# Graph network, last two layers: steps of 50 places in five blocks, and edge jobs spread over more groups

## The chip, the cores and the metric

One core of a Trainium2 chip runs the whole program. The metric is device microseconds of one execution, the median of several. Before the change it is 16802.36 us (three executions, 16799.04 to 16803.32).

## The reference

12500 nodes with 48 features pass four graph layers over the same 400000 edges (sorted by destination); each layer's result is added to the features and normalized.

```
x = ln(x + L0)   # message MLP on [x_dst, x_src, edge], summed over dst
x = ln(x + L1)   # x_src * deg^-1/2, summed over dst, linear, relu
x = ln(x + L2)   # deg^-1/2 scaled x_dst, summed over SRC, linear, relu
x = ln(x + L3)   # gate(edge) * x_dst * cutoff * mult, summed over SRC, divided
# gate(edge) = silu(edge_attr_40 @ W1 + b1) @ W2 + b2 + adapt(edge)
```

The last two layers sum over the source node, by which the edges are not sorted.

## The kernel before, in words

The edges are cut into 125 groups of 3200 (25 tiles of 128, in five chunks). Layers 0 and 1 (`pass0`, `pass1`) go over them once each. `pass0` also counts how many edges go to each block of 128 source nodes, one count for each of six *parts* of the groups (`GROUPS`). `pass1` works out a place for every edge in a table `order` in DRAM, in which, part by part, the edges of one block of nodes lie together. The places are read later in *steps* of `RT` = 40, a place being 128 rows; for each step DVE works out which blocks of nodes its places belong to (`block_no`, called numbering here, L1179 to L1181, once for each of the first 40 groups, and L1265 to L1270 after them).

Layers 2 and 3 are both `scatter_pass` (L1570). For each group:

- SP loads ids, five windows of the node table and the edge data (`load_edges`).
- DVE builds one-hots of the destinations (L1825); PE looks the 25 tiles up with 25 small matmuls (L1940, `look_up`).
- ACT (`begin`) writes the message tile and the places (L2030 to L2032) once the scatters of the same chunk of the group before have landed; DVE multiplies (`take`: L1844 in layer 2, L1841 in layer 3). In layer 3 ACT makes the gates of reading groups itself, 25 activations (L2020), from coefficients of DVE (L1814, L1817).
- POOL scatters the 25 tiles to `order` (L1757), one indirect DMA each.

The first part (40 groups) does this and, beside it, the *jobs*: a job is the gate network over one group of 3200 edges (PE L1913 and L1920, ACT L1992 and L1999, stored to `gates`). `GATES2` and `GATES3` say for each layer how many groups carry two jobs (*pairs*), how many carry one (*singles*), and the first job. The pass asserts that the jobs take `GROUPS[0] - 1` groups. Layer 2 makes jobs 0 to 77 in 39 groups, layer 3 makes 78 to 124 in 8 + 31.

From the second part on, each group also reads one step (*reading groups*): SP loads the step's places, one DMA for each block of 10 places (`load_order`, L1685), each after PE has reduced the same block of the step before. DVE builds the one-hots of a block (`block_digits`, L1789), PE reduces the ten places into one of two PSUM banks, `red[b % 2]` (`block_reduce`: L1904 clears, L1906 multiplies), and DVE adds the bank to the node sums (`block_sums`, L1803). DVE's order in a group is: one-hots for the look-up, the sum of the last block of the step before, then the five products, with a block's one-hots built behind each of the first four, then the other sums. PE does the look-up and then the step's blocks. The first group of each part is a *head*: SP waits until all scatters of the parts before have landed, then loads; DVE builds after all products. When the groups are through, the steps that are left (nine) run as a *tail*.

Of the kernel before, what the change touches and what calls it, by code (L numbers as in the profile page):

```python
# [41 lines left out]
MW = F + 1  # L42
# [2 lines left out]
BANK = 512  # L45
AHEAD = 3
ROUND_BIT = 512
GROUPS = (40, 28, 20, 15, 12, 10)
PARTS = len(GROUPS)
OW = MW + 1  # L50
RB = (10, 10, 10, 10)
LINE = 16
RT = sum(RB)
TEN = RB[0]
RUN = 10
GATES2 = (39, 0, 0)
GATES3 = (8, 31, 78)


class Plan:  # L60


    def __init__(self, n, e):
# [7 lines left out]
        assert self.NR <= ROUND_BIT  # L71
        assert sum(GROUPS) == self.NG
        self.begin = [sum(GROUPS[:q]) for q in range(PARTS)]
        self.TAIL = -(-(GROUPS[-1] * GT + self.NB) // RT)
        self.steps = GROUPS[1:] + (self.TAIL,)
        self.step0 = [sum(self.steps[:q]) for q in range(PARTS)]
        assert all(n * GT + self.NB <= k * RT for n, k in zip(GROUPS, self.steps))
        self.NS = sum(self.steps)
# [22 lines left out]
def bc(ap, shape):  # L101
    return ap.to_broadcast(shape)


def gnn(nc, a, out):
# [4 lines left out]
    def dram(name, shape, dt=F32):  # L110
# [16 lines left out]
        order=dram("order", [P * pl.TT, OW]),  # L127
        blocks=dram("blocks", [pl.NS, len(RB) + 1, LINE], I32),
    )
# [826 lines left out]
def pass1(nc, pl, a, d, r, ps):  # L956
# [5 lines left out]
    NG, NB, TT, HB = pl.NG, pl.NB, pl.TT, pl.HB  # L962
    MOST = max(pl.steps)
    ADDS = SC + DT
    assert GROUPS[0] == RT
    hacc = ps[0:F, 0:SC * WN].rearrange("p (c n) -> p c n", n=WN)
    cumf = ps[:, BANK:BANK + CT * NB]
    cum = cumf.rearrange("p (t b) -> p t b", b=NB)
# [9 lines left out]
    with Stage(nc, "l1") as s:  # L978
# [33 lines left out]
        block_no = s.sb("block_no", [MOST, PARTS, RT])  # L1012
        blk = s.sb("blk", [MOST, PARTS, len(RB) + 1, LINE], I32)
        first_of = s.sb("first_of", [MOST, PARTS * len(RB)])
        zero = s.sb("zero", [P, pl.ZT * OW])
# [12 lines left out]
        blk_ready, blk_out = s.sem("blk_ready"), s.sem("blk_out")  # L1028
        first_found, blk_made = s.sem("first_found"), s.sem("blk_made")
# [67 lines left out]
        def _(dve):  # L1097
            v = nc.vector
# [60 lines left out]
                    more = hacc[:, i, :] if i < SC else packed[:, (i - SC) * WD:(i - SC + 1) * WD]  # L1159
                    v.tensor_tensor(cols, cols, more, ALU.add).then_inc(acc_added, 1)  # L1160

            def group(g, part):
                mine = ids[:, ds(g % 2, 1), :, :].rearrange("p o t k -> p (o t) k")
                dve.wait_ge(ids_in, (g + 1) * 16)
                dve.nop(nofuse=True)
# [9 lines left out]
                v.scalar_tensor_tensor(near[:, :], nodes[:, ST:GT], 16.0, r["dbase"][:, ds(g, 1), :].rearrange("p o t -> p (o t)"), ALU.mult, ALU.subtract).then_inc(self_id, 1)  # L1175
                v.scalar_tensor_tensor(far[:, 0:ST].rearrange("p (c t) -> p c t", t=CT), nodes[:, 0:ST].rearrange("p (c t) -> p c t", t=CT), 4.0,
                                       bc(base4[:, ds(g, 1), :].rearrange("p o c -> p c o"), [P, SC, CT]), ALU.mult, ALU.subtract).then_inc(self_id, 1)
                if part == 0:
                    v.tensor_tensor(begun[:, :, :], first_tile[0:MOST, :, :], bc(tile_no[0:MOST, ds(g, 1)].rearrange("p (q o) -> p q o", o=1), [MOST, PARTS, NB]), ALU.is_le).then_inc(self_blk, 1)  # L1179
                    dve.wait_ge(self_blk, g + 1)  # L1180
                    v.tensor_reduce(block_no[:, :, ds(g, 1)].rearrange("p q o -> p (q o)"), begun[:, :, :], AX, ALU.add).then_inc(blk_ready, 1)  # L1181
# [76 lines left out]
                dve.wait_ge(self_shift, last * 2 + 3)  # L1258

            dve.wait_ge(lone_set, len(batches))  # L1260
            for part in range(PARTS):
                if part == 1:
                    dve.wait_ge(blk_ready, RT)
                    tens = block_no[:, :, :].rearrange("p q (b k) -> p (q b) k", k=TEN)
                    v.tensor_scalar(first_of[:, :], tens[:, :, 0], float(MW), None, ALU.mult).then_inc(first_found, 1)  # L1265
                    dve.wait_ge(first_found, 1)
                    for q in range(PARTS):
                        mine = slice(q * len(RB), (q + 1) * len(RB))
                        v.scalar_tensor_tensor(blk[:, q, 0:len(RB), 0:TEN], tens[:, mine, :], float(MW), bc(first_of[:, mine].rearrange("p (b o) -> p b o", o=1), [MOST, len(RB), TEN]), ALU.mult, ALU.subtract)
                        v.tensor_scalar(blk[:, q, len(RB), 0:len(RB)], first_of[:, mine], float(-MW), None, ALU.add).then_inc(blk_made, 1)  # L1270
                    dve.wait_ge(blk_made, PARTS)
                    dve.sem_inc(blk_ready, 1)
                with dve.Fori(pl.begin[part], pl.begin[part] + GROUPS[part]) as g:
                    group(g, part)
            with dve.Fori(NG - 1, NG) as g:
                _bodies, _before, last = load_bodies(dve, "dve", pl, r, g)
                add_sums(last + 1)
# [292 lines left out]
def scatter_pass(nc, pl, a, d, r, ps, layer):  # L1570
# [7 lines left out]
    NG, NB, NT, TT = pl.NG, pl.NB, pl.NT, pl.TT  # L1578
# [3 lines left out]
    HE = EV * P  # L1582
    pairs, singles, job0 = (GATES3 if gated else GATES2)
    JOBS = pairs + singles
# [23 lines left out]
    STEP = len(RB)  # L1608
# [3 lines left out]
    with Stage(nc, f"l{layer}") as s:  # L1612
# [10 lines left out]
        blk = s.sb("blk", [1, 2, STEP + 1, LINE], I32)  # L1623
# [19 lines left out]
        ohs_ready, red_ready, agg_added = s.sem("ohs_ready"), s.sem("red_ready"), s.sem("agg_added")  # L1643
# [245 lines left out]
        @block.tensor  # L1889
        def _(pe):  # L1890
            t = nc.tensor
            pe.sem_inc(look_ready, 5)
            pe.sem_inc(win_used, 2)
            pe.sem_inc(red_ready, len(RB))
            pe.sem_inc(z_ready, 2 * NCH)
            pe.wait_ge(zeros_set, 1)

            def block_reduce(n, b):
                pe.wait_ge(ohs_ready, n * len(RB) + b + 1)
                pe.wait_ge(ord_in[b], (n + 1) * 16)  # L1900
                pe.wait_ge(blk_in, (n + 2) * 16)
                slots = load_slots(pe, "slot", r, blk, n, b)
                pe.wait_ge(agg_added, n * STEP + b + STEP)
                t.matmul(red[b % 2], none[:, 0:P], none[:, :], start=True, stop=False, skip_group_check=True)  # L1904
                for k in range(TEN):
                    done = t.matmul(red[b % 2][:, ds(slots[k], MW)], ohs[b][:, k, :],  # L1906
                                    ordb[b][:, k, 0:MW], start=False, stop=False, skip_group_check=True)
                done.then_inc(red_ready, 1)

            def make_hidden(g, many, i):  # L1910
                pe.wait_ge(ea_in[i // NCH][i % NCH], (g + 1) * 16)
                pe.wait_ge(sil_ready, item0(g, many) + i + 1)
                t.matmul(zps, w1[:, :], eat[:, i // NCH, i % NCH, :], start=True, stop=True).then_inc(z_ready, 1)  # L1913

            def make_gates(g, many, i):
                pe.wait_ge(sil_ready, item0(g, many) + i + 2)
                pe.wait_ge(made_copied, item0(g, many) + i + 1)
                for q in range(EV):
                    wide = F * min(2, CT - 2 * q)
                    done = t.matmul(gps[:, 2 * q * F:2 * q * F + wide], sil[:, i % 2, q * P:(q + 1) * P], w2[:, 0:wide], start=True, stop=True)  # L1920
                done.then_inc(made_ready, 1)

            def jobs(g, many):
                make_hidden(g, many, 0)
                for i in range(many * NCH):
                    if i + 1 < many * NCH:
                        make_hidden(g, many, i + 1)
                    make_gates(g, many, i)

            def look_up(g):  # L1930
                _starts, rounds, before, last_round = load_group(pe, "pe", pl, r, g)
                with pe.Fori(0, rounds) as k:
                    w = before + k
                    n = w * NCH
                    pe.wait_ge(win_in, (w + 1) * 16 * NCH)
                    for c in range(NCH):
                        pe.wait_ge(oht_ready, n + c + 1)
                        pe.wait_ge(look_zero, g * NCH + c + 1)
                        for j in range(CT):
                            done = t.matmul(look[c][:, j, :], oht[:, c * CE + j * P:c * CE + (j + 1) * P],  # L1940
                                            win[:, ds((w % 2) * SET + c * LW, LW)], start=False, stop=False, skip_group_check=True)
                        done.then_inc(look_ready, 1)
                    pe.wait_ge(look_ready, n + NCH + 5)
                    pe.sem_inc(win_used, 1)

            with pe.Fori(0, 1) as g:
                look_up(g)
            pe.wait_ge(w_in, 8 * 16)
            for begin, end, many in spans:
                with pe.Fori(begin + 1, end + 1) as g:  # L1950
                    look_up(g)
                    jobs(g - 1, many)
            assert JOBS + 1 == READ0
            pe.wait_ge(made_copied, (2 * pairs + singles) * NCH + 1)
            with pe.Fori(READ0, NG) as g:
                look_up(g)
                for b in range(len(RB)):
                    block_reduce(g - READ0, b)
            with pe.Fori(NG - READ0, pl.NS) as n:
                for b in range(len(RB)):  # L1960
                    block_reduce(n, b)
# [486 lines left out]
```

## Time and profile before

| what | value |
|---|---|
| median of the runs | 16802.36 us |
| profiled execution, its own time | 16791.52 us |
| its span | 16789.7 us |
| PE, PEld (share of the span) | 69%, 57% |
| DVE, ACT | 52%, 23% |
| POOL | 66% |
| mean granted clock | 0.661 |

Layer 2 goes from about 7815 to 12224 us of the span, layer 3 from about 12310 to 16700. The shares are averages over four layers and their epilogues, so the rows below are taken stretch by stretch. A timeline row gives the start of an instruction and, in brackets, how long its engine was idle before it and what released it.

### The profile page before, as it was taken

To read this page: it belongs to the slowest core of one execution; us is meant where nothing else is said; L and a number is where in the kernel's file an instruction comes from. 1 tells how busy PE (TensorE), PEld (TensorE's weight loads), DVE (VectorE), ACT (ScalarE), POOL (GpSimd) and SP (SyncE) were. 2 spreads that over 40 slices of the span, in tenths; PEclk is the share of its full clock that TensorE was granted. 3 is DMA by queue.
4 is the path that set the end of the run, shared out by engine and by line. 5 is a ranking of instruction groups with operands and counts; after the bars stand their busy time and mean duration, and the time that the engine had idled before them with its cause. 6 is when DMAs were issued, how large, how long until landed. Compare 5 with 4: busy or idle time off the path is not lost. (4 is left out here: it accounts for less than half of the span.)

```text
span 16789.7 us, 290124 instructions
## 1 busy us (share of the span) xinstructions
PE 11513.4 (69%) x64352; PEld 9568.8 (57%) x64353; DVE 8750.1 (52%) x19588; ACT 3873.3 (23%) x10408; POOL 11073.3 (66%) x11400
## 2 busy tenths in 40 slices
PE   7877877877666666665777766666755446666666
PEld 6777777777444444444555666566643336565555
DVE  4666666666677666664111444444432234444444
ACT  1111111111222222223444211111022223333331
POOL 4777777777545555555666777777546777777773
PEclk9999999999766666665555555555555555555555
DMA  5444444443111111112333333333223333333331
GB/s 130 101 101 101 101 100 101 102 101 91 47 40 43 45 46 44 46 44 76 110 110 110 95 87 87 86 84 90 71 77 92 94 92 95 88 96 92 92 92 51
DMA packets 1579142, 1406.93 MB, mean 84 GB/s; under 512 B 987004, under 2 KB 1445903, under 8 KB 1574658
## 3 DMA queue, kind: packets, MB, share of 16 engines
q1 hardware_dynamic: 601532, 636.68, 14.5%
q0 software_dynamic: 410000, 462.80, 11.0%
q10 hardware_dynamic: 567508, 306.27, 6.6%
q8 instruction: 42, 0.69, 0.0%
q14 instruction: 60, 0.49, 0.0%
HBM read 984.49 MB, written 420.17 MB: 84 GB/s over the span
## 5 line engine op out<-in xcount | busy, mean ns | idle before, releaser
L1757 POOL DMA_INDIRECT order<-l_msg,l_uring x6250 | 6069.5, 971 | 2356.7 <-issue 1831.9
L547 POOL DMA_INDIRECT l_rows<-btab,l_sd x3125 | 2993.7, 958 | 1128.3 <-issue 1087.2
L1906 PEld LDWEIGHTS ps<-l_ordb,l_ohs 128*128 128x128 f32 x15040 | 3263.7, 331 | 313.8 <-issue 313.8
L1906 PE MATMUL ps<-l_ordb,l_ohs 128*128 128x49 f32 x15040 | 3385.3, 415 | 0.0
L1086 POOL DMA_INDIRECT l_rows<-y,l_sd x1875 | 1822.0, 972 | 1621.5 <-DMA l_sd<-in_sd 1087.9
L688 PE MATMUL ps<-l_rhs,l_lhs 64*128 x6250 | 1421.9, 424 | 666.5 <-DVE l_rows L624 466.5
L688 PEld LDWEIGHTS ps<-l_rhs,l_lhs 64*128 64x128 f32 x6250 | 1350.8, 328 | 728.1 <-issue 728.1
L1904 PE MATMUL ps<-l_none 1*128 1x490 bf16 x752 | 438.0, 582 | 1694.4 <-DVE l_ohs L1789 1143.1
L1071 ACT ACTIVATE l_adj<-ps 128x588 f16<-128x588 f32 x1260 | 784.0, 664 | 2636.3 <-PE ps L1315 2629.0
L703 PEld LDWEIGHTS ps<-l_ohe,l_hid 128*128 128x128 f32 x6250 | 1342.8, 332 | 34.7 <-issue 34.0
L703 PE MATMUL ps<-l_ohe,l_hid 128*128 128x32 f32 x6250 | 1359.8, 402 | 0.6 <-ACT l_hid L733 0.6
L733 ACT ACTIVATE l_hid<-l_rows 128x640 f32<-128x640 f32 x625 | 460.4, 737 | 3509.6 <-DVE l_rows L624 3509.6
L1940 PE MATMUL ps<-l_win,l_oht 96*128 x6250 | 474.8, 243 | 1158.7 <-DVE l_oht L1825 912.9
L1334 PEld LDWEIGHTS ps<-l_adj,yhm 128*96 128x96 f16 x12348 | 941.3, 173 | 545.9 <-DVE acc L1160 408.0
L1315 PE MATMUL ps<-l_okey,l_hlo 128*128 128x294 bf16 x2520 | 680.7, 390 | 795.2 <-DVE l_okey L1202 636.8
L1803 DVE TENSOR_TENSOR acc<-acc,ps 128x490 f32 x752 | 500.9, 666 | 1328.9 <-PE ps L1906 1170.9
L1334 PE MATMUL ps<-l_adj,yhm 128*96 128x60 f16 x12348 | 940.3, 247 | 345.6 <-DVE acc L1160 345.6
L1920 PEld LDWEIGHTS ps<-l_w,l_sil 97*128 97x128 f32 x3750 | 924.8, 329 | 440.5 <-issue 382.4
L1789 DVE TENSOR_TENSOR l_ohs<-ps,l_ordb 128x1280 f32<-128x1280 f32 x752 | 1113.1, 1481 | 69.7 <-DMA l_ordb<-order 69.5
L1844 DVE TENSOR_TENSOR l_prod<-ps,l_esr 128x160 f32<-128x160 f32 x625 | 200.8, 322 | 1819.2 <-ACT l_uring L2032 1685.5
L1940 PEld LDWEIGHTS ps<-l_win,l_oht 96*128 96x128 bf16 x6250 | 401.4, 132 | 1240.3 <-issue 1238.0
L1904 PEld LDWEIGHTS ps<-l_none 1*128 1x128 bf16 x752 | 74.0, 98 | 1782.9 <-issue 1223.0
(317 smaller groups left out, 15842.4 us busy)
## 6 DMA issues: line engine op xcount, KB each, us to landing
l_ordb<-order SPq DMA_DIRECT2D x752, 250.0 KB
l_dstb<-ids SPq DMA_DIRECT2D x250, 600.0 KB
order<-l_msg,l_uring POOLq DMA_INDIRECT x6250
order<-l_zero ACTq DMA_DIRECT2D x125, 775.0 KB
l_eat<-in_ea40P SPq DMA_DIRECT2D x625, 120.0 KB, 2.1
gates<-l_made ACTq DMA_DIRECT2D x625, 120.0 KB
l_gin<-gates SPq DMA_DIRECT2D x125, 600.0 KB
l_rows<-btab,l_sd POOLq DMA_INDIRECT x3125
```

Source lines behind the costliest of these rows:

```text
L547: pool.indirect_dma_start(rows[:, t, :], None, d["btab"], bass.IndirectOffsetOnAxis(ap=sd[:, t, 0:1], axis=0)).then_inc(gat[c], 16)
L688: last = t.matmul(pre[c % 2][:, j * P:(j + 1) * P], lhs[:, c * CE + j * P:c * CE + (j + 1) * P], window, start=True, stop=True)
L703: last = t.matmul(hacc[:, c, :], hid[:, c * CT + j, :], ohe[:, c * CT + j, :], start=(j == 0), stop=(j == CT - 1))
L1071: nc.scalar.activation(adj[:, :, t * WD:(t + 1) * WD].rearrange("p (h n) d -> p h n d", n=HB), pair[t % 2].rearrange("p h (n d) -> p h n d ...
L1086: pool.indirect_dma_start(rows[:, slot, t, :], None, d["y1"], bass.IndirectOffsetOnAxis(ap=sd[:, slot, t, 0:1], axis=0)).then_inc(gat[c], 16)
L1315: done = t_.matmul(pair[t % 2][:, h, :], hlo[:, t % BUILT, :], okey[:, t % BUILT, h * HB * WD:(h + 1) * HB * WD], start=True, stop=True)
L1334: done = t_.matmul(packed, r["yhm"][:, b, :], adj[:, b, :], start=(b == 0), stop=(b == NB - 1))
L1757: pool.indirect_dma_start(d["order"], bass.IndirectOffsetOnAxis(ap=uring[:, t:t + 1], axis=0), msg[:, t, :], None).then_inc(sc[c], 16)
L1789: v.tensor_tensor(ohs[b][:, :, :], bc(count_row[:, None, :], [P, RB[b], P]), bc(lo, [P, RB[b], P]), ALU.is_equal).then_inc(ohs_ready, 1)
L1906: done = t.matmul(red[b % 2][:, ds(slots[k], MW)], ohs[b][:, k, :], ordb[b][:, k, 0:MW], start=False, stop=False, skip_group_check=True)
L1920: done = t.matmul(gps[:, 2 * q * F:2 * q * F + wide], sil[:, i % 2, q * P:(q + 1) * P], w2[:, 0:wide], start=True, stop=True)
L1940: done = t.matmul(look[c][:, j, :], oht[:, c * CE + j * P:c * CE + (j + 1) * P], win[:, ds((w % 2) * SET + c * LW, LW)], start=False, stop ...
```

## The change

The constants become `GROUPS = (54, 29, 17, 11, 8, 6)`, `RB` five blocks of 10, so `RT` = 50, `GATES2 = (19, 34, 0)` and `GATES3 = (0, 53, 72)`.

- Layers 2 and 3 have 54 groups before reading in place of 40, and 71 reading groups in place of 85, each with a step of five blocks; the steps of the parts are 29, 17, 11, 8, 6 and 5 (76 in all; 94 before: 28, 20, 15, 12, 10 and 9), so the tail has five steps in place of nine. A layer reads 380 blocks in place of 376.
- Layer 2 makes 72 jobs: 19 groups with two, 34 with one. Layer 3 makes 53, one a group.
- The fifth block's one-hots are built behind the fifth product. As the number of blocks is now odd, the first block of a step has the same bank as the last of the step before, and PE waits for one more sum there.
- There is one more buffer for places and one for one-hots.
- `pass1` numbers the first 50 groups, and DVE's loop over the groups is split there alone and no longer at every part.

```diff
--- before.py
+++ after.py
@@ -45,16 +45,16 @@
 BANK = 512
 AHEAD = 3
 ROUND_BIT = 512
-GROUPS = (40, 28, 20, 15, 12, 10)
+GROUPS = (54, 29, 17, 11, 8, 6)
 PARTS = len(GROUPS)
 OW = MW + 1
-RB = (10, 10, 10, 10)
+RB = (10, 10, 10, 10, 10)
 LINE = 16
 RT = sum(RB)
 TEN = RB[0]
 RUN = 10
-GATES2 = (39, 0, 0)
-GATES3 = (8, 31, 78)
+GATES2 = (19, 34, 0)
+GATES3 = (0, 53, 72)
 
 
 class Plan:
@@ -962,7 +962,7 @@
     NG, NB, TT, HB = pl.NG, pl.NB, pl.TT, pl.HB
     MOST = max(pl.steps)
     ADDS = SC + DT
-    assert GROUPS[0] == RT
+    assert RT <= GROUPS[0]
     hacc = ps[0:F, 0:SC * WN].rearrange("p (c n) -> p c n", n=WN)
     cumf = ps[:, BANK:BANK + CT * NB]
     cum = cumf.rearrange("p (t b) -> p t b", b=NB)
@@ -1159,7 +1159,7 @@
                     more = hacc[:, i, :] if i < SC else packed[:, (i - SC) * WD:(i - SC + 1) * WD]
                     v.tensor_tensor(cols, cols, more, ALU.add).then_inc(acc_added, 1)
 
-            def group(g, part):
+            def group(g, numbering):
                 mine = ids[:, ds(g % 2, 1), :, :].rearrange("p o t k -> p (o t) k")
                 dve.wait_ge(ids_in, (g + 1) * 16)
                 dve.nop(nofuse=True)
@@ -1175,7 +1175,7 @@
                 v.scalar_tensor_tensor(near[:, :], nodes[:, ST:GT], 16.0, r["dbase"][:, ds(g, 1), :].rearrange("p o t -> p (o t)"), ALU.mult, ALU.subtract).then_inc(self_id, 1)
                 v.scalar_tensor_tensor(far[:, 0:ST].rearrange("p (c t) -> p c t", t=CT), nodes[:, 0:ST].rearrange("p (c t) -> p c t", t=CT), 4.0,
                                        bc(base4[:, ds(g, 1), :].rearrange("p o c -> p c o"), [P, SC, CT]), ALU.mult, ALU.subtract).then_inc(self_id, 1)
-                if part == 0:
+                if numbering:
                     v.tensor_tensor(begun[:, :, :], first_tile[0:MOST, :, :], bc(tile_no[0:MOST, ds(g, 1)].rearrange("p (q o) -> p q o", o=1), [MOST, PARTS, NB]), ALU.is_le).then_inc(self_blk, 1)
                     dve.wait_ge(self_blk, g + 1)
                     v.tensor_reduce(block_no[:, :, ds(g, 1)].rearrange("p q o -> p (q o)"), begun[:, :, :], AX, ALU.add).then_inc(blk_ready, 1)
@@ -1258,20 +1258,20 @@
                 dve.wait_ge(self_shift, last * 2 + 3)
 
             dve.wait_ge(lone_set, len(batches))
-            for part in range(PARTS):
-                if part == 1:
-                    dve.wait_ge(blk_ready, RT)
-                    tens = block_no[:, :, :].rearrange("p q (b k) -> p (q b) k", k=TEN)
-                    v.tensor_scalar(first_of[:, :], tens[:, :, 0], float(MW), None, ALU.mult).then_inc(first_found, 1)
-                    dve.wait_ge(first_found, 1)
-                    for q in range(PARTS):
-                        mine = slice(q * len(RB), (q + 1) * len(RB))
-                        v.scalar_tensor_tensor(blk[:, q, 0:len(RB), 0:TEN], tens[:, mine, :], float(MW), bc(first_of[:, mine].rearrange("p (b o) -> p b o", o=1), [MOST, len(RB), TEN]), ALU.mult, ALU.subtract)
-                        v.tensor_scalar(blk[:, q, len(RB), 0:len(RB)], first_of[:, mine], float(-MW), None, ALU.add).then_inc(blk_made, 1)
-                    dve.wait_ge(blk_made, PARTS)
-                    dve.sem_inc(blk_ready, 1)
-                with dve.Fori(pl.begin[part], pl.begin[part] + GROUPS[part]) as g:
-                    group(g, part)
+            with dve.Fori(0, RT) as g:
+                group(g, True)
+            dve.wait_ge(blk_ready, RT)
+            tens = block_no[:, :, :].rearrange("p q (b k) -> p (q b) k", k=TEN)
+            v.tensor_scalar(first_of[:, :], tens[:, :, 0], float(MW), None, ALU.mult).then_inc(first_found, 1)
+            dve.wait_ge(first_found, 1)
+            for q in range(PARTS):
+                mine = slice(q * len(RB), (q + 1) * len(RB))
+                v.scalar_tensor_tensor(blk[:, q, 0:len(RB), 0:TEN], tens[:, mine, :], float(MW), bc(first_of[:, mine].rearrange("p (b o) -> p b o", o=1), [MOST, len(RB), TEN]), ALU.mult, ALU.subtract)
+                v.tensor_scalar(blk[:, q, len(RB), 0:len(RB)], first_of[:, mine], float(-MW), None, ALU.add).then_inc(blk_made, 1)
+            dve.wait_ge(blk_made, PARTS)
+            dve.sem_inc(blk_ready, 1)
+            with dve.Fori(RT, NG) as g:
+                group(g, False)
             with dve.Fori(NG - 1, NG) as g:
                 _bodies, _before, last = load_bodies(dve, "dve", pl, r, g)
                 add_sums(last + 1)
@@ -1900,7 +1900,7 @@
                 pe.wait_ge(ord_in[b], (n + 1) * 16)
                 pe.wait_ge(blk_in, (n + 2) * 16)
                 slots = load_slots(pe, "slot", r, blk, n, b)
-                pe.wait_ge(agg_added, n * STEP + b + STEP)
+                pe.wait_ge(agg_added, n * STEP + b + STEP + (1 if b == 0 and STEP % 2 else 0))
                 t.matmul(red[b % 2], none[:, 0:P], none[:, :], start=True, stop=False, skip_group_check=True)
                 for k in range(TEN):
                     done = t.matmul(red[b % 2][:, ds(slots[k], MW)], ohs[b][:, k, :],
```

## Rows read from the trace of the kernel before

**Rows 1.** Stretches: busy us (count) by engine, granted clock, DMA share, GB/s.

```profile
10500.00:11500.00 1000.00, 683.92 (x3421) 609.85 (x3420) 462.67 (x657) 155.36 (x633) 760.35 (x787) 0.50 0.32 87
15000.00:16000.00 1000.00, 673.14 (x3415) 595.10 (x3414) 455.88 (x685) 368.76 (x1336) 755.98 (x782) 0.50 0.34 92
```

**Rows 2.** Waits, layer 2 reading: us in total, times, longest.

```profile
ACT l_msg L2030 <- DMA order<-l_msg,l_uring: 1017.6, 234, 6.8
```

**Rows 3.** Timeline of POOL (start, us, what, idle before): scatters.

```profile
8530.64 0.97 POOL L1757 DMA_INDIRECT order<-l_msg,l_uring  x1 [2.57 <-ACT l_uring L2032]
...
9335.37 0.97 POOL L1757 DMA_INDIRECT order<-l_msg,l_uring  x1 [7.00 <-ACT l_uring L2032]
...
12035.52 0.97 POOL L1757 DMA_INDIRECT order<-l_msg,l_uring  x1 [0.30 <-issue]
...
13794.09 0.97 POOL L1757 DMA_INDIRECT order<-l_msg,l_uring  x1 [7.96 <-ACT l_uring L2032]
...
16511.08 0.97 POOL L1757 DMA_INDIRECT order<-l_msg,l_uring  x1 [0.30 <-issue]
```

**Rows 4.** Timeline of PE, layer 2: look-ups, two jobs between.

```profile
8528.75 1.86 PE L1940 MATMUL ps<-l_win,l_oht 96*128 x25 [7.46 <-DVE l_oht L1825]
...
8566.90 1.85 PE L1940 MATMUL ps<-l_win,l_oht 96*128 x25 [7.32 <-DMA l_win<-y]
```

**Rows 5.** Timeline of PE, layer 3: look-ups, two jobs between.

```profile
12536.28 0.39 PE L1940 MATMUL ps<-l_win,l_oht 96*128 x5 [16.29 <-DVE l_oht L1825]
...
12583.55 0.39 PE L1940 MATMUL ps<-l_win,l_oht 96*128 x5 [16.11 <-DVE l_oht L1825]
```

**Rows 6.** Timeline of PE, layer 3: look-ups, one job between.

```profile
13304.16 0.39 PE L1940 MATMUL ps<-l_win,l_oht 96*128 x5 [15.42 <-DVE l_oht L1825]
...
13338.27 0.39 PE L1940 MATMUL ps<-l_win,l_oht 96*128 x5 [15.41 <-DVE l_oht L1825]
```

**Rows 7.** Timeline of PE, layer 2: look-ups of groups behind a head.

```profile
9364.48 1.99 PE L1940 MATMUL ps<-l_win,l_oht 96*128 x25
...
9390.59 2.18 PE L1940 MATMUL ps<-l_win,l_oht 96*128 x25
```

**Rows 8.** Timeline of PE, layer 3: blocks 0, 0 and 1 behind a head.

```profile
13799.36 0.58 PE L1904 MATMUL ps<-l_none 1*128 1x490 bf16 x1 [10.66 <-DVE l_ohs L1789]
...
13828.95 0.58 PE L1904 MATMUL ps<-l_none 1*128 1x490 bf16 x1 [7.10 <-DVE l_ohs L1789]
...
13833.90 0.58 PE L1904 MATMUL ps<-l_none 1*128 1x490 bf16 x1
```

**Rows 9.** Timelines of ACT and DVE, layer 3: gates, first product.

```profile
13816.93 8.05 ACT L2020 ACTIVATE l_gate<-l_gin,l_cwa,l_cwg 128x48 f32 x25 [10.83 <-DVE l_cwa L1817]
...
13825.28 0.41 DVE L1841 TENSOR_TENSOR l_msg<-ps,l_gate 128x245 f32<-128x245 f32 x1 [2.90 <-ACT l_uring L2032]
```

**Rows 10.** Timeline of SP's queue, layer 2: first load of the tail.

```profile
12038.34 0.59 SPq L1681 DMA_DIRECT2D l_blk<-blocks  x1
```

**Rows 11.** Timelines of SP, PE, PE and POOL, layer 3: a head group.

```profile
14686.94 0.27 SPq L1681 DMA_DIRECT2D l_blk<-blocks  x1
...
14693.47 0.58 PE L1904 MATMUL ps<-l_none 1*128 1x490 bf16 x1 [24.28 <-DVE l_ohs L1789]
...
14713.12 0.69 PE L1940 MATMUL ps<-l_win,l_oht 96*128 x10
...
14720.99 0.96 POOL L1757 DMA_INDIRECT order<-l_msg,l_uring  x1 [3.73 <-ACT l_uring L2032]
```

**Rows 12.** Page, costliest groups: busy, mean ns, idle before.

```profile
L1803 DVE TENSOR_TENSOR acc<-acc,ps 128x490 f32 x752 | 500.9, 666 | 1328.9 <-PE ps L1906 1170.9
...
L1789 DVE TENSOR_TENSOR l_ohs<-ps,l_ordb 128x1280 f32<-128x1280 f32 x752 | 1113.1, 1481 | 69.7 <-DMA l_ordb<-order 69.5
```

**Rows 13.** Stretches, layer 1, DVE's line L1244 alone: ten groups each.

```profile
5073.70:5352.40 278.70, 26.99 (x10) 0.65 0.16 43
5464.60:5733.50 268.90, 27.00 (x10) 0.63 0.16 45
```

## The prediction

> **What bounds the kernel now.** I read the busy shares of stretches first, then each engine's timeline for the repeating group of 3200 edges, then the waits. In both reading stretches (groups that scatter messages and also reduce one step of the order) the granted clock is 0.50, the lower level (1.2 GHz), in layer 2 and in layer 3 alike; POOL issues 787 and 782 scatters per 1000 us, 31.8 and 32.0 us for the 25 of a group [rows 1]. In layer 2 ACT waits 234 times for a scatter's landing before it may write the message tile again [rows 2]: the others run ahead and are held back by POOL. From first to last scatter of the 85 reading groups POOL takes 2700.2 us in layer 2 (31.78 a group) and 2717.0 us in layer 3 (31.98, with the idle of the heads below) [rows 3]. Where jobs are made, POOL is not the bound: from look-up to look-up a group takes 38.15 us with two jobs in layer 2 [rows 4], 47.27 (47.0 over the eight) with two in layer 3 [rows 5], and 34.11 (34.15 over the thirty) with one in layer 3 [rows 6].
>
> What the others need when POOL does not hold them back shows right behind a head group. Layer 2: 26.11 from look-up to look-up [rows 7]. Layer 3: 29.59 from first block to first block, 4.95 between blocks [rows 8]. Layer 3 needs more because the loop goes through ACT: DVE's sum of the last but one block, coefficients, 25 gate activations (8.05 us) on ACT, the first product on DVE, its one-hots, PE's first block [rows 8, 9]. This loop has 2.3 us to spare in layer 3 and 5.7 in layer 2. The change adds a fifth block to it.
>
> **Layer 3, term by term.** (a) Jobs: eight groups of 47.0 go, 22 of 34.15 come: -376.0 + 751.3 = +375.3 us until reading begins. (b) The reading loop: one block more before the sum that starts the next group: 29.75 (mean of some thirty such groups) + 4.95 = 34.70 us. That is above POOL's 32: POOL now waits about 2.8 us in each group. (c) Heads, the first group of each part: SP holds the order loads until all earlier scatters have landed. The last scatter's end to SP's first load is 1.85 us (12036.49 to 12038.34) [rows 3, 10]; SP to the first block 6.53, four blocks 19.65 to the next look-up, 7.87 from there to POOL's first scatter [rows 11]. With five blocks: 31.57 (25 scatters) + 1.85 + 6.53 + 24.60 + 7.87 = 72.4 us over two groups where the loop alone gives 69.4: 3.0 us a head. The four-block head already shows POOL idle for 3.73 [rows 11], which this sum gives as 3.7. (d) Reading after: 70 intervals of 34.70, five heads of 3.0, the last group's 31.6: 2475.6 against 2717.0, -241.4. (e) Tail: before, nine steps of four blocks, 36 x 4.95 = 178.1 us; after, five of five, 25 x 4.95 = 123.7. The number of blocks to a step becomes odd, so block 0 uses the bank of the last block of the step before, and PE must wait for its sum: 0.67 us [rows 12]. The trace has no such wait; between 0 (hidden) and 2 us (three sums' length) I take 0.93, the sum and an estimated quarter to see it, as in the tail nothing lies between; behind it on PE stand all further blocks, and DVE's sums wait for them. Four times: +3.7. Together -50.7. Within reading the same wait costs nothing: DVE does that sum before it builds the one-hots for which block 0 waits in any case; were this cover gone, 0.9 us for each of 71 groups, 66 us a layer where PE bounds. Layer 3: +375.3 - 241.4 - 50.7 = **+83.2 us**.
>
> **Layer 2.** (a) Twenty groups with two jobs go: -763.0. (b) 34 groups with one job come, a form that layer 2 does not have in the trace. Below, POOL's 31.78 bounds them (nothing can pass it); above, the layer 3 form at 34.15. That one is a loop through the gates loaded for the next group (loads, cutoff activations, coefficients), which layer 2 has not; five jobs fewer are worth 12.9 us in layer 3 (47.0 against 34.11), so layer 2's own loop would want about 38.15 - 12.9 = 25.3. I take 31.78: +1080.5, and 2.2 us once (0 to 4, an estimate), as the first of them finds its second chunk late. (c) Before reading, the wait for the stored gates leaves POOL idle 7.00 against 2.57 in a pair group [rows 3]; behind single groups POOL has nearly a group in hand and this goes: -4.4. (d) Fourteen reading groups go: -444.9. (e) The reading loop becomes 26.11 + 4.95 = 31.06, under 31.78 by 0.7: POOL keeps the bound, thinly. (f) Heads: SP's first load to the next look-up is 6.53 + 24.60, and 1.89 to POOL [rows 3, 4], 33.0 us; POOL is free after 31.78 + 0.30 - 1.85 = 30.2: 2.8 us idle, five times, +14.0 (none with four blocks). (g) Tail -50.7. Layer 2: **-166.3 us**.
>
> The fifth load of 250 KB a step is issued by SP once PE has reduced the same block of the step before, a whole group ahead of its use. DMA share is 0.32 to 0.34 [rows 1], so a quarter more of these loads finds room; if it did not, a step would start late as it does at heads, where the loads are open: 6.53 us.
>
> **Layer 1.** Numbering runs for the first 50 groups in place of 40. DVE's ten groups take 278.7 us with it and 268.9 without [rows 13]: 0.98 a group, +9.8. PE has a loop of its own for the last group of an odd part; three parts are odd in place of one: between 0 and 6 us, I take 3. **+12.8 us**. Layer 0 keeps its six parts and its work: 0.
>
> **Sum.** -166.3 + 83.2 + 12.8 = -70.3. The profiled execution took 16791.5 (span 16789.7), so 16721.2; the median shown is 10.8 higher, so **16732 us**, 0.4% faster.
>
> **Rivals.** (A) POOL stays the bound in layer 3 as well. For it: no engine is busier there, POOL 756 against PE 673 and DVE 456 of 1000 us [rows 1]. Against it: the loop behind heads repeats at 29.6 to 30.0 with no engine full, and POOL is already idle at heads. Then 71 groups at 31.98, 2270.6 in place of 2475.6: 205 us less, 16527 us. The Trainium skill's Perfetto Trace Analysis, section Identifying the Most-Contended Engine, says the engine with the highest occupancy is the most contended and is to be optimized first; by that, work added to PE and DVE is free, which is this rival. The rows of layer 2 agree with it, those behind the heads of layer 3 do not. (B) Slower: the loop grows by more than a block, because the fifth one-hot build now stands between the last product and the first sum (1.48 us [rows 12]), and the bank wait of 0.93 is not covered. Layer 3 then goes with 37.1 us and layer 2 with 33.5: 70 x 2.4 + 71 x 1.7 = +289, 17021 us. For it: in steady state PE's third block waits for exactly that first sum. Against: PE has two blocks (9.9 us) in hand while DVE gets there. It decides from 1.0 us a group in layer 3 alone (70 us over 70 groups). (C) Layer 2's single groups are held by their loads at 34.15: 34 x 2.37 = +81, 16813 us, no change.
>
> **How the numbers follow.** Forecast 0.70, its own range 16695 to 16770 (0.3 us a group in the layer 3 loop is 21 us; layer 2's transitions 10; layer 1's odd loops 3; 10 between executions). A 0.06, B 0.09, C 0.08; the rest, 0.07, are mixtures just above the forecast. The range that leaves out A and most of B, but holds C: 16665 to 16820. What this measurement can tell from no change is 0.2%, 34 us, so the borders are 16769 and 16836. Faster: 0.68 of the forecast, A, 0.02 of the rest, 0.76. Same: C and the forecast's edge, 0.15. Slower: 0.09.
>
> **What would show it.** In the profile after: look-ups of layer 3's reading groups 34.7 apart and POOL idle about 2.8 us before each group's first scatter; layer 2's 31.8 apart with only heads showing POOL idle; layer 2's groups 20 to 53 at 31.8; PE's tails 127 us. Wrong would be: layer 3 at 32 (A), layer 2 above 32.5 (B) or at 34 before reading (C).

## The result and the profile after

The kernel after takes 16707.27 us (median of 5 runs, 16700.66 to 16713.0), the kernel before, beside it, 16799.04 us (16794.38 to 16803.32): a ratio of 0.9945, 95% interval 0.993 to 0.996. The forecast was 16732 in a range of 16665 to 16820, so the time lies 25 us below it and inside the range. The profiled execution spans 16698.9 us against 16789.7: 90.8 us less, where the sum of the prediction had 70.3.

The page after, its span and its busy shares:

```profile
span 16698.9 us, 289908 instructions
PE 11607.6 (70%) x64520; PEld 9620.9 (58%) x64521; DVE 8794.7 (53%) x19652; ACT 3819.4 (23%) x10108; POOL 11083.6 (66%) x11400
```

The shares say nothing of where the time went; the same two stretches as in [rows 1] do:

```profile
10500.00:11500.00 1000.00, 823.81 (x4024) 737.07 (x4024) 511.07 (x711) 152.75 (x620) 756.35 (x784) 0.50 0.34 94
15000.00:16000.00 1000.00, 750.11 (x3714) 666.00 (x3713) 473.58 (x687) 343.67 (x1242) 694.10 (x717) 0.50 0.34 93
```

In layer 2 POOL still issues 784 scatters per 1000 us (787 in [rows 1]), though PE has 824 us of work there in place of 684. In layer 3 it issues 717 in place of 782: a group takes 34.9 us here on average, heads included, where it took 32.0. The granted clock is 0.50 in both, the lower level, as before.

From PE's timeline in layer 2, two look-ups before reading and two behind a head:

```profile
9029.06 0.51 PE L1940 MATMUL ps<-l_win,l_oht 96*128 x5 [7.55 <-DVE l_oht L1825]
...
9060.85 0.51 PE L1940 MATMUL ps<-l_win,l_oht 96*128 x5 [7.57 <-DVE l_oht L1825]
...
9722.50 1.58 PE L1940 MATMUL ps<-l_win,l_oht 96*128 x20
...
9753.54 1.54 PE L1940 MATMUL ps<-l_win,l_oht 96*128 x20
```

A group with one job takes 31.79 us: POOL's pace. Behind a head, where POOL does not hold it back, a reading group takes 31.04; in [rows 7] it was 26.11.

From POOL's timeline, the first scatter of reading, a first group behind a head, and the last scatter of layer 2; then the first of reading, two group starts and the last of layer 3 (before: [rows 3]):

```profile
9659.02 0.97 POOL L1757 DMA_INDIRECT order<-l_msg,l_uring  x1 [0.30 <-issue]
...
9693.25 0.97 POOL L1757 DMA_INDIRECT order<-l_msg,l_uring  x1 [2.76 <-ACT l_uring L2032]
...
11926.45 0.97 POOL L1757 DMA_INDIRECT order<-l_msg,l_uring  x1 [0.30 <-issue]
...
13999.96 0.97 POOL L1757 DMA_INDIRECT order<-l_msg,l_uring  x1 [8.13 <-ACT l_uring L2032]
...
14071.94 0.97 POOL L1757 DMA_INDIRECT order<-l_msg,l_uring  x1 [3.19 <-ACT l_uring L2032]
...
14106.66 0.97 POOL L1757 DMA_INDIRECT order<-l_msg,l_uring  x1 [3.18 <-ACT l_uring L2032]
...
16471.40 0.97 POOL L1757 DMA_INDIRECT order<-l_msg,l_uring  x1 [0.31 <-issue]
```

Layer 2 reads for 2267.4 us (before 2700.2), layer 3 for 2471.4 (before 2717.0). In layer 3 POOL waits 3.2 us before every reading group outside heads (0.3 in before). One turn of layer 3's loop, from the timelines of DVE, ACT and PE (the block that starts at 14059.50 is the fifth of its step):

```profile
14061.99 0.19 DVE L1817 TENSOR_TENSOR l_cwa<-l_cwg,adapt 128x25 f32<-128x25 f32 x1
...
14071.09 1.48 DVE L1789 TENSOR_TENSOR l_ohs<-ps,l_ordb 128x1280 f32<-128x1280 f32 x1
...
14062.41 8.05 ACT L2020 ACTIVATE l_gate<-l_gin,l_cwa,l_cwg 128x48 f32 x25 [15.85 <-DVE l_cwa L1817]
...
14039.72 0.58 PE L1904 MATMUL ps<-l_none 1*128 1x490 bf16 x1 [7.49 <-DVE l_ohs L1789]
...
14059.50 0.58 PE L1904 MATMUL ps<-l_none 1*128 1x490 bf16 x1
14064.32 0.62 PE L1940 MATMUL ps<-l_win,l_oht 96*128 x10
...
14074.43 0.58 PE L1904 MATMUL ps<-l_none 1*128 1x490 bf16 x1 [7.49 <-DVE l_ohs L1789]
```

PE has the look-up done by about 14067 and then stands for 7.49 us, ACT had stood for 15.85 us before its gates: neither is full, each waits for the other through DVE. The first block of this step started at 14039.72, that of the next at 14074.43, so a turn is 34.71 us, and the rows account for all of it: four blocks on PE 19.78, the sum and the coefficients 2.91, the gates 8.05, and 3.97 for the first product, its one-hots and the start of PE's block. The look-up lies beside the gates.

### The profile page after: what moved, and what is told of

Read it like the earlier page. It is cut to its first block and busy times, and to the rows that moved or that the text cites. A ratio compares the mean times of both kernels' runs of the same rounds, so it can differ in the third digit from the quotient of the medians.

```text
span 16698.9 us, 289908 instructions
## 1 busy us (share of the span) xinstructions
PE 11607.6 (70%) x64520; PEld 9620.9 (58%) x64521; DVE 8794.7 (53%) x19652; ACT 3819.4 (23%) x10108; POOL 11083.6 (66%) x11400
## 5 line engine op out<-in xcount | busy, mean ns | idle before, releaser
L1906 PEld LDWEIGHTS ps<-l_ordb,l_ohs 128*128 128x128 f32 x15200 | 3298.2, 331 | 317.1 <-issue 317.1
L1906 PE MATMUL ps<-l_ordb,l_ohs 128*128 128x49 f32 x15200 | 3421.1, 415 | 0.0
L703 PEld LDWEIGHTS ps<-l_ohe,l_hid 128*128 128x128 f32 x6250 | 1342.8, 332 | 34.7 <-issue 34.0
L1789 DVE TENSOR_TENSOR l_ohs<-ps,l_ordb 128x1280 f32<-128x1280 f32 x760 | 1124.8, 1481 | 37.2 <-DMA l_ordb<-order 36.8
L1913 PE MATMUL ps<-l_eat,l_w 80*96 80x384 f32 x1250 | 987.6, 894 | 198.4 <-ACT l_sil L1992 125.3
L1825 DVE TENSOR_TENSOR l_oht<-ps,l_dstb 96x640 bf16<-96x640 f32 x1250 | 936.2, 812 | 188.1 <-DMA l_dstb<-ids 98.4
```

The source lines that it names most:

```text
L703: last = t.matmul(hacc[:, c, :], hid[:, c * CT + j, :], ohe[:, c * CT + j, :], start=(j == 0), stop=(j == CT - 1))
L1789: v.tensor_tensor(ohs[b][:, :, :], bc(count_row[:, None, :], [P, RB[b], P]), bc(lo, [P, RB[b], P]), ALU.is_equal).then_inc(ohs_ready, 1)
L1825: v.tensor_tensor(oht[:, chunk_edges(c)], bc(nid[:, c:c + 1], [WK, CE]), dstb[:, ds((g % 2) * GE + c * CE, CE)], ALU.is_equal).then_inc(oh ...
```

## The experiments

All kernels but e2 are edits of the kernel after. e1 to e4 ran on one chip, on which the kernel before takes 16809.6 us. The other three batches came to three other chips, on which it takes 23940 (e5 to e8), 24112 (f1 to f3) and 23935 us (g1); the times of a batch can be set only against runs of the same batch and that kernel, which ran in each. The times expected for them, but for a few said to be for the slow chip, were worked out for a chip like the first, so they are not tested; what is tested is how look-ups move.

**e1: ACT's gates out of the loop.**

```
# DVE, reading groups of layer 3; coefs(g) is the lines of cwg and cwa, which leave the
# start of the group; ... marks what is left out
...
+                        if gated and ahead and b == 1:
+                            coefs(g + 1)
                         block_sums(n, b)
...
# in heads the same two lines stand ahead of block_digits(n, b + 1)
```

> The kernel after, with one change in layer 3's reading groups: DVE computes the coefficients of the next group behind its first sum of a step, not behind the fourth, so the 25 gate activations no longer stand in the loop sum, coefficients, gates, product, one-hots, block 0. My theory (this loop sets layer 3's 34.7 us a group, POOL could do 31.8): the look-ups of layer 3's reading groups come to 31.8 apart, POOL's idle before each first scatter goes except at heads, its 71 reading groups take 70 x 31.78 + 5 x 2.8 + 31.6 = 2270 in place of 2472 us, and the kernel 16707 - 202 = 16505 us (16485 to 16530). Rival 1 (five blocks need this time on PE, in the loads of the order or in the one-hots, and the gates only fill a gap): look-ups stay at 34.7, 16707 us. Rival 2 (part of it): another wait, near 33, 16600 us.

Measured: 16547.71 us (16538.81 to 16549.93), 0.9846 of before (0.983 to 0.9863). That is 0.99% of the old time, about 166 us, under the kernel after, each taken against its own runs of before. PE's look-ups behind a head, ACT's gates in the group between, and what the head itself shows on PE, DVE and POOL:

```profile
15034.63 1.23 PE L1950 MATMUL ps<-l_win,l_oht 96*128 x20
...
15053.15 8.05 ACT L2030 ACTIVATE l_gate<-l_gin,l_cwa,l_cwg 128x48 f32 x25 [0.98 <-DVE l_cwa L1812]
...
15065.30 1.26 PE L1950 MATMUL ps<-l_win,l_oht 96*128 x20
...
14958.51 0.58 PE L1914 MATMUL ps<-l_none 1*128 1x490 bf16 x1 [5.14 <-issue]
...
14955.09 0.19 DVE L1809 SCALAR_TENSOR_TENSOR l_cwg<-l_under,l_cut 128x25 f32<-128x25 f32 x1 [5.85 <-ACT l_cut L1998]
...
14976.75 0.97 POOL L1757 DMA_INDIRECT order<-l_msg,l_uring  x1 [9.58 <-issue]
```

The same gates now lie beside PE's blocks, and the free loop is 30.67 us in place of 34.7. POOL's 31.8 is the bound again. The 8.05 us of gates give back 4.0 and not 8: from the end of the last sum but one to the first product it is 10.38 us in after and 6.34 in e1, since DVE's one-hots of the look-up (3.74 us) now stand where the gates stood. The time missed my 16505 by 43 us and lies above its range (to 16530), and the rows say where: my edit made a wait of its own. In a head DVE asks for the next group's cutoff before it builds the third block's one-hots, but SP loads the distances for it only behind the head's order loads; DVE stands 5.85 us, PE's third block 5.14, and POOL is idle for 9.58, 9.79, 9.90 and 10.41 us at four heads, some 28 us more than the 2.8 each of the sum. The groups before reading took 34.22 in this run and not 34.01: 11 us. The two make 39 of the 43.

**e2: the same edit with four blocks** (in the kernel before).

> The same edit in the kernel before (four blocks). My theory (with four blocks the loop is 29.75 and POOL's 31.78 the bound): only the 3.7 us of POOL idle at each of the heads of layer 3 can go, 5 x 3.7 = 19 us: 16780 us, look-ups 31.8 apart as before. Rival (layer 3's reading was bound by the loop before too): 85 groups get shorter by more than 1 us, under 16700 us.

Measured: 16807.24 us (16802.6 to 16826.01), ratio 1.000 (0.9991 to 1.001), where 16780 was expected. PE's look-ups behind a head, and POOL at that head:

```profile
14768.97 0.83 PE L1950 MATMUL ps<-l_win,l_oht 96*128 x15
...
14794.88 0.83 PE L1950 MATMUL ps<-l_win,l_oht 96*128 x15
...
14746.80 0.97 POOL L1757 DMA_INDIRECT order<-l_msg,l_uring  x1 [4.42 <-issue]
```

The free loop falls from 29.6 to 25.9 us, and nothing comes of it, since POOL had been the bound at 31.8 all along. The 19 us expected at heads stayed away too: POOL's idle there is 4.4 to 5.1 us, by the same new wait as in e1, and not 0.

With e1 this makes a table of the free loop of a reading group in layer 3, in us:

| | four blocks | five blocks | a block adds |
|---|---|---|---|
| gates in the loop | 29.6 (before) | 34.7 (after) | 5.1 |
| gates beside it | 25.9 (e2) | 30.7 (e1) | 4.8 |
| the gates cost | 3.7 | 4.0 | |

Only one of the four lies above POOL's 31.8, and it is the kernel after.

**e3: the larger step alone.**

```
-GROUPS = (54, 29, 17, 11, 8, 6)
+GROUPS = (40, 28, 20, 15, 12, 10)
...
-GATES2 = (19, 34, 0)
-GATES3 = (0, 53, 72)
+GATES2 = (39, 0, 0)
+GATES3 = (8, 31, 78)
...
-    assert RT <= GROUPS[0]
```

> The step of five blocks alone: the kernel after with the groups 40, 28, 20, 15, 12, 10 and the jobs' numbers of the kernel before, so 85 groups read and the steps are partly empty. My theory: layer 3's reading goes from 2717 to 84 x 34.65 + 5 x 2.4 + 31.6 = 2954 us, +237; tail of 7 steps of five blocks (35) for 9 of four (36), +1; layer 2 keeps POOL's 31.78 and gets 2.8 us at each of five heads and 1 in the tail, +15; layer 1 +7: 16799 + 260 = 17059 us. Rival A (the fifth block is free under POOL in both layers): +20, 16819 us. Rival B (the loop grows by more than a block): layer 3 above 36, over 17170 us.

Measured: 17073.75 us (17064.69 to 17082.47), ratio 1.0157 (1.014 to 1.0174), 264 us slower than before where 260 were expected. Two look-ups of layer 3:

```profile
15021.95 0.62 PE L1939 MATMUL ps<-l_win,l_oht 96*128 x10
...
15056.67 0.62 PE L1939 MATMUL ps<-l_win,l_oht 96*128 x10
```

34.72 apart; layer 2's free look-ups are 30.7 to 31.0 apart, and from its first look-up to that of layer 3 it takes 4539 us, where the kernel before has 4506. So a fifth block by itself is a loss; by the table of terms further down, what makes the change a gain are the fourteen fewer groups that pay for blocks at all, and the shorter tails. A first part of 54 groups with steps of four blocks was not run, so what that part is worth without the fifth block stays open.

**e4: the jobs packed as before.**

```
-GATES2 = (19, 34, 0)
-GATES3 = (0, 53, 72)
+GATES2 = (39, 0, 0)
+GATES3 = (8, 31, 78)
...
# and loops of PE and ACT for the groups from JOBS + 1 up to READ0, without a job
```

> The kernel after with the jobs as they were before: layer 2 two jobs in each of groups 0 to 38 and none in 39 to 53, layer 3 two in each of 0 to 7, one in 8 to 38 and none in 39 to 53. My theory: layer 2 pays 20 x (38.15 - 31.78) = +127 us, layer 3 8 x (47.0 - 34.0) - 14 x (34.0 - 31.8) = +73 us: 16707 + 200 = 16907 us, slower than the kernel before. Groups without a job in layer 3 then show 31.8 from look-up to look-up (a rival: 34 there too, by the loads and not by the job; then 16940). Rival: spreading the jobs is worth nothing by itself, 16707 us.

Measured: 16918.58 us (16915.34 to 16921.96), ratio 1.0067 (1.005 to 1.0084), so 1.2% (some 205 us) over the kernel after, and slower than the kernel before. Layer 3's groups without a job:

```profile
13833.33 0.39 PE L1940 MATMUL ps<-l_win,l_oht 96*128 x5 [28.89 <-DMA l_win<-htab]
...
13865.49 0.39 PE L1940 MATMUL ps<-l_win,l_oht 96*128 x5 [28.92 <-DMA l_win<-htab]
```

They are 32.2 apart, and POOL is idle for no more than 0.31 us before any of their scatters (of 0.98 us each): without a job POOL sets the pace in layer 3 as well. Spreading the jobs is the half of the change without which it would lose.

**e5: the fifth one-hots built later.**

```
-                    if reading and not head and c <= LAST:
+                    if reading and not head and c < LAST:
                         block_digits(n, c)
 ...
                         block_sums(n, b)
+                        if b == 0:
+                            block_digits(n, LAST)
```

> The kernel after, but in reading groups the one-hots of the fifth block are built behind DVE's first sum and not between the last product and that sum. My theory (the build, 1.48 us, ends when PE's block 0 of the step ends, and costs nothing): look-ups stay 34.7 apart in layer 3 and the time stays at 16707 us (+-10). Rival B (the fifth build delays the first sum, by it PE's third block, and so the loop): 1 us or more a group comes back in layer 3, under 16640 us.

Measured: 24464.98 us (24411.94 to 24472.63), 1.022 of before (1.0203 to 1.0237) on that chip. As a test of rival B this run settles nothing, for the kernel after did not run there. This part of B is settled by rows of the kernel after, DVE in two successive groups:

```profile
14043.24 1.48 DVE L1789 TENSOR_TENSOR l_ohs<-ps,l_ordb 128x1280 f32<-128x1280 f32 x1
14045.11 0.67 DVE L1803 TENSOR_TENSOR acc<-acc,ps 128x490 f32 x1 [0.39 <-PE ps L1906]
...
14077.95 1.48 DVE L1789 TENSOR_TENSOR l_ohs<-ps,l_ordb 128x1280 f32<-128x1280 f32 x1
14079.59 0.67 DVE L1803 TENSOR_TENSOR acc<-acc,ps 128x490 f32 x1 [0.16 <-PE ps L1906]
```

Behind the fifth build DVE still waits, 0.39 and 0.16 us, for PE's block 0: the build fits, with almost nothing to spare.

**e6 and f3: more gates in the loop** (the same kernel twice).

```
# ACT, reading groups of layer 3
                         make_gates(c)
+                        if c == 0:
+                            make_gates_again()   # five more, into a tile of their own
```

> The kernel after with five more gate activations on ACT in each of layer 3's 71 reading groups, behind the first five; their results go to a tile that nobody reads. Each takes 0.32 us, 1.6 us a group. My theory (ACT's gates stand in the loop that sets 34.7 us): though ACT is busy for a third of this stretch only, 71 x 1.6 = +114 us: 16821 us, look-ups 36.3 apart. But only chunk 0's gates stand between coefficients and the first product if DVE may start with it; as the extra ones stand right behind chunk 0's, the first product may go ahead and only the later ones slip: then less, at the least 0. Rival (PE's blocks or the loads of the order set 34.7): 16707 us.

> The kernel of e6 (after, with five more gate activations in each of layer 3's reading groups) once more. On a chip where the kernel before takes 16800: 71 x 1.61 = +114 us against after, 16821 us, look-ups 36.3 apart (the late chip showed 56.7 for 55.0, +1.65); rival (not ACT's gates but PE's blocks or the loads set 34.7): 16707 us.

Measured: 24564.34 us (24538.15 to 24574.72), 1.0257 (1.024 to 1.0274), 99 us over e5 on the same chip, and in the other batch 24631.91 us, 1.0216 (1.0199 to 1.0233). Two look-ups of layer 3, of e5 and then of e6:

```profile
21328.59 1.12 PE L1939 MATMUL ps<-l_win,l_oht 96*128 x15
...
21383.71 1.12 PE L1939 MATMUL ps<-l_win,l_oht 96*128 x15
```

```profile
21301.26 1.12 PE L1941 MATMUL ps<-l_win,l_oht 96*128 x15
...
21357.97 1.12 PE L1941 MATMUL ps<-l_win,l_oht 96*128 x15
```

55.1 and 56.7. Over 22 groups the means are 54.96 and 56.69, 1.73 apart; over all reading groups outside heads they are 54.95 and 56.48, 1.53 apart: about the five gates (1.61). So ACT's gates lie in the loop that sets the pace there as well, though it is 20 us longer on that chip. One thing is mixed in: e5 stands for the kernel after, from which it differs by the place of the fifth build, and what that is worth there no run shows. That the first product might leave early did not happen: it also waits for chunk 0's indices, which ACT writes in begin(0), behind all gates.

**e7 and f1: heads mended** (again one kernel).

```
# DVE, heads of layer 3; reading groups as in e1
                         block_digits(n, b + 1)
+                        if gated and ahead and b == LAST - 1:
+                            coefs(g + 1)
                         block_sums(n, b)
```

> Early coefficients as in e1, but in head groups DVE computes them ahead of its fourth sum and not of the third block's one-hots. In e1 DVE waited 5.85 us at a head for the next group's cutoff, whose load SP issues only behind the head's order loads, with PE's third block behind it, and POOL was idle for 9.6 to 10.4 us at four of the heads. My theory: that wait goes, POOL is idle for about 2.8 us at a head as in layer 2, 16548 - 5 x 7 = 16513 us (16500 to 16530). Rival (the heads are long because PE's blocks and the loads need that): 16548 us.

> The kernel of e7 (early coefficients, at heads ahead of the fourth sum) once more, since e5 to e8 ran on a chip whose transfers land so much later that the kernel before takes 23940 us there. On a chip where it takes 16800: 16513 us (16500 to 16530), look-ups of layer 3's reading groups 31.8 apart on average, POOL idle for about 2.8 us at a head. On the late chip: 24186 us again.

Measured: 24186.07 us (24136.86 to 24189.91), 1.0103 (1.0086 to 1.012), 279 us under e5; and 24268.65 us, 1.0067 (1.005 to 1.0083). Reading groups are 51.2 apart where e5 has 55.0: 3.8 us, the price of the gates in the table again. Whether the mended head brings the 35 us over e1 was not measured on a chip like that of e1 and stays open.

**e8, f2 and g1: the distances loaded early as well** (one kernel, three batches).

```
# e7, and in load_edges, right behind the load of dstb (the old load of dist goes)
+                if gated:
+                    sp.dma_start(dist[...], a["dist"][...]).then_inc(dist_in, 16)
...
# ACT's cut_weights; SP waits for dist_in too, behind its loads
-                act.wait_ge(edge_in, (g + 1) * EDGE)
+                act.wait_ge(dist_in, (g + 1) * 16)
```

> As e7, and in layer 3 the distances of a group are loaded ahead of its windows under a semaphore of their own, so that cutoff, coefficients and the look-up's one-hots no longer wait for the gates' load behind the windows. My theory (groups that make one job in layer 3 take 34.0 because of that chain, POOL would do 31.8): look-ups of groups 1 to 53 come to 31.8 apart, 53 x 2.2 = -117 us against e7: 16396 us (16380 to 16430). Rival (they are held by the job's own chain through PE and ACT, or by the windows' load): 34 stays, 16513 us.

> The kernel of e8 (the distances loaded early as well) once more. On a chip where the kernel before takes 16800: groups 1 to 53 of layer 3 at 31.8 in place of 34.0, 53 x 2.2 = 117 us less than f1: 16396 us (16380 to 16430); rival (the job's chain or the windows' load holds them): no difference to f1. On the late chip they went from 55.6 to 47.6.

> The kernel of e8 and f2 (after, with early coefficients and early distances in layer 3) for a chip where the kernel before takes 16800. Against e1 (16548): POOL's idle at heads falls from 10 to about 2.8 us, 5 x 7 = -35 us, and groups 1 to 53 of layer 3 go from 34.2 to 31.8 apart, 53 x 2.4 = -127 us: 16386 us, ratio 0.975 (0.973 to 0.980). Rival for the second term (the job's chain or the windows' load holds these groups at 34): 16513 us, ratio 0.983. On the late chip again 0.995 to 0.997.

Measured: 23811.95 us, 0.9946 (0.9929 to 0.9963); 24041.69 us, 0.997 (0.9959 to 0.9982); 23813.85 us, 0.9942 (0.9925 to 0.9959). Look-ups of layer 3's groups with one job, of e7 and then of e8:

```profile
18941.50 0.39 PE L1950 MATMUL ps<-l_win,l_oht 96*128 x5 [23.41 <-DVE l_oht L1828]
...
18996.02 0.39 PE L1950 MATMUL ps<-l_win,l_oht 96*128 x5 [20.50 <-DVE l_oht L1828]
```

```profile
18777.57 1.69 PE L1955 MATMUL ps<-l_win,l_oht 96*128 x25 [25.76 <-DMA l_win<-htab]
...
18825.05 1.67 PE L1955 MATMUL ps<-l_win,l_oht 96*128 x25 [26.61 <-DMA l_win<-htab]
```

54.5 and 47.5 us (means 55.3 and 47.6; 53.5 and 47.7 from the twentieth group on in f1 and f2): PE no longer waits for one-hots that stand behind the cutoff, but for the windows. So on these chips the chain of loads and cutoff does hold these groups, against the rival; what is left is the windows' load, which the rival had named too. On a chip like that of e1, where POOL's 31.8 would be the floor, it wasn't measured. For the slow chip g1 expected 0.995 to 0.997 and got 0.9942, with 0.995 inside the interval.

Of the kernels tried, e1 is the fastest where before takes 16800 us (0.9846, against the 0.9945 of the kernel after). On the three other chips the one of e8, by 0.3 to 0.6%, is the only one that beats before; the kernel after itself did not run on them.

## Why the prediction was right

Term by term, from the profiled executions, in us:

| | predicted | measured |
|---|---|---|
| layers 0 and 1 (to layer 2's first look-up) | +12.8 | +7.2 |
| layer 2 until reading | +315.3 | +316.4 |
| layer 2 reading, heads with it | -430.9 | -432.7 |
| layer 2 tail | -50.7 | -50.8 |
| layer 3 until reading | +375.3 | +365.7 |
| layer 3 reading | -241.4 | -245.6 |
| layer 3 tail | -50.7 | -51.2 |
| sum | -70.3 | -90.8 |

The terms are rounded one by one. Until reading is from the first look-up to POOL's first scatter of a reading group, reading from there to the last scatter, tail all behind it.

- **Layer 2's single groups**, the form that no row of before showed: 31.79 us, POOL's pace. Rival C (34.15) is dead, and the loop of their own that I had put at 25.3 by subtraction shows: the first of them, before POOL holds them back, are 25.04, 24.84 and 25.78 us apart.
- **The loop of layer 3**: 34.70 predicted, 34.55 to 34.79 read outside heads. Rival A would have had 31.98; e1 shows that the price of the loop and no other hindrance keeps layer 3 from it, and gives back 166 of the 205 us that separated A from the forecast. By the Trainium skill's Perfetto Trace Analysis, section Identifying the Most-Contended Engine, which has the engine of highest occupancy optimized first, POOL was the engine to look at. Layer 2's rows agree with that, at 787 scatters per 1000 us before the change and 784 behind it, though PE was then busy for 824 us and POOL for 756; layer 3's do not, at 782 and 717.
- **Rival B** (the build between product and sum, and the bank wait): the build fits (e5's rows), and the bank wait appears in the tail alone. From PE's timeline there, the last block of one step and the first of the next:

```profile
11955.96 0.58 PE L1904 MATMUL ps<-l_none 1*128 1x490 bf16 x1
11961.84 0.58 PE L1904 MATMUL ps<-l_none 1*128 1x490 bf16 x1 [0.87 <-DVE acc L1803]
```

5.88 us in place of 4.95, so 0.93, which is the value taken.
- **Heads**: layer 2's 2.8 us of POOL idle reads 2.76. Layer 3's 3.0 were too many: look-ups across a head are 36.8 to 37.1 apart, 2.1 to 2.4 over the loop.
- **Sizes that were off**, all on the side that made the kernel faster: layer 3's groups before reading (34.15 predicted, mean 34.01; from the first look-up to the second it is 3.4 us shorter, 16.7 with one job in place of 20.2 with two, and 20.3 again in e4; with the passage into reading 9.6 in all), layer 1 (5.6 too many; which of its two parts, numbering or PE's odd loops, wasn't tried), and the heads. They make the 20 us between the sums. The other 4 of the 25 are the step from profile to median: I added 10.8, and it was 6.6.
- **Two slips that move nothing.** The "five jobs fewer" worth 12.9 us are one job fewer, of five chunks. The check on the four-block head, given as 3.7, is 3.9 by its terms (67.5 over two groups of 31.78), against the 3.73 read.

## What to carry to other kernels

Before work is added to an engine that is not full, find out what it does between its waits: a group that closes a loop through several engines paid for each block in full here (5.1 and 4.8 us for one of 4.95), however idle the engines looked, and the place to read that is where the slowest engine has just been emptied. Two layers with the same code can lie on both sides of the bound, and the sum has to be made for each. Taking 8 us of work out of such a loop gave back 4, because other work moved into its place. And when work is taken out, look at the places where the load it needs is late, since that is where the new wait comes, as at the heads of e1.

## What was not expected

**The chip matters more than the change.** Three of four batches came to chips on which the kernel before takes 42 to 44% longer. Durations of the engines' instructions are the same (a scatter on POOL 971 ns in e5 and 973 in after, a reduction matmul 413 and 415), and it isn't the granted clock (0.649 and 0.662 on average). What differs stands between instructions. SP's two loads of a group that follow one another with no wait between them, in after and in e5:

```profile
14040.90 0.37 SPq L1701 DMA_DIRECT2D l_dist<-in_dist  x1
14041.50 0.34 SPq L1702 DMA_DIRECT2D l_gin<-gates  x1
```

```profile
22881.64 0.71 SPq L1701 DMA_DIRECT2D l_dist<-in_dist  x1
22885.19 0.69 SPq L1702 DMA_DIRECT2D l_gin<-gates  x1
```

0.60 us apart and 3.55, and SP's own time for an issue is 0.34 to 0.37 us and 0.69 to 0.71. In the expectations I had put this down to transfers that land later; these rows don't bear that out. The cutoff that waits for the second of these loads starts 3.9 us behind its issue in after and 2.2 in e5.

Most of the 20 us by which a group is longer stand before DVE's first sum of a step, where after has 0.39 us (the row under e5). In e5, POOL's last scatter of a group and that sum:

```profile
22907.49 0.97 POOL L1757 DMA_INDIRECT order<-l_msg,l_uring  x1 [0.30 <-issue]
22908.65 0.67 DVE L1803 TENSOR_TENSOR acc<-acc,ps 128x490 f32 x1 [25.69 <-DMA btab<-pro_stb]
```

By PE's timeline the block to be summed had ended at 22884.4, 24 us earlier. (The transfer that the row names is a store from the kernel's beginning, and this sum does not wait for it.) Such a stand, 20.5 us long on average (10.0 to 27.3), comes in every one of layer 3's 71 reading groups (in eight of them twice) and ends near the end of POOL's scatters, from 10 us before it to 4 behind. POOL takes 31.6 us for its 25 scatters as in after, and then pauses for 23.4 us where after has 3.2: what lay beside the scatters on the first chip now comes in large part behind them. Why, and whether it is the chip or something else about those batches, no run here shows.

For the change it means that its gain is shown only where before takes 16800 us. e5, which differs from it by the place of one build, is 2.2% slower than before on such a chip, where the reading groups of layer 3 take 55.0 us in place of 34.7.
